# Graph network kernel: four fixed edge tiles for each of the 30 keys of the three-relation graph, counted without loops

## The reference

```python
seg = edge_type * n + dst
agg = jax.ops.segment_sum(x[src], seg, num_segments=N_REL * n)
cnt = jax.ops.segment_sum(ones, seg, num_segments=N_REL * n)
mean = agg.reshape(N_REL, n, -1) / jnp.maximum(cnt, 1.0).reshape(N_REL, n, 1)
h1 = jnp.einsum('rni,rio->no', mean, W_rel) + x @ W_root + b_rgcn
...
# three-relation layers: message of each edge, by relation
onehot = jax.nn.one_hot(edge_type, NUM_REL, dtype=h.dtype)
count = jax.ops.segment_sum(onehot, dst, num_segments=num_nodes)
inv = jnp.where(count > 0, 1.0 / jnp.maximum(count, 1.0), 0.0)
msg = xw[edge_type, src] * inv[dst, edge_type][:, None]
agg = jax.ops.segment_sum(msg, dst, num_segments=num_nodes)
```

## Time and profile before

| what | us |
|---|---|
| median of 3 runs | 1991.13 (1988.38 to 1992.34) |
| the profiled execution: its own time | 1990.38 |
| its span, first to last instruction | 1988.7 |
| 17 list units (262 to 586) | first loop of the block |
| 15 key units (588.3 to 990.6) | 402.2 |

### The profile page before, as it was taken

The page is one execution under the profiler, slowest core; times in us unless marked ns, Lnnn a source line. Parts: engine busy times, 40 slices in busy tenths (PEclk is TensorE's granted clock), DMA queues, the critical chain, the costliest instruction groups (busy, mean ns, idle before and its releaser), DMA issues. The chain is left out here.

```text
span 1988.7 us, 31024 instructions
## 1 busy us (share of the span) xinstructions
PE 1710.9 (86%) x10102; PEld 1570.3 (79%) x10103; DVE 1150.2 (58%) x1890; ACT 629.2 (32%) x839; POOL 352.4 (18%) x301
## 2 busy tenths in 40 slices
PE   2765279999989888888873998999998999899988
PEld 1643269899878777777763898899998999899988
DVE  7979777777766545555563646355343455444463
ACT  3000135565554444444443221222112222222220
POOL 5020136456452322222230000000000000000000
PEclk9876589999999989989995999899998999999999
DMA  4000249798885666666564111222012221231111
GB/s 151 24 17 0 85 156 271 209 270 261 213 260 160 157 166 183 191 174 185 162 165 120 47 49 53 81 81 72 22 55 72 72 71 32 58 84 55 50 47 47
DMA packets 84489, 230.08 MB, mean 116 GB/s; under 512 B 10350, under 2 KB 22641, under 8 KB 84434
## 3 DMA queue, kind: packets, MB, share of 16 engines
q1 hardware_dynamic: 65090, 158.14, 25.0%
q0 software_dynamic: 19344, 71.18, 15.5%
HBM read 190.01 MB, written 39.28 MB: 115 GB/s over the span
## 5 line engine op out<-in xcount | busy, mean ns | idle before, releaser
L923 PE MATMUL layers_ps_o<-layers_w_hi,layers_g_hi 128*125 128x384 f32 (+1 forms) x1040 | 362.4, 348 | 4.5 <-DVE layers_w_lo L787 3.2
L924 PE MATMUL layers_ps_o<-layers_w_lo,layers_g_hi 128*125 128x384 f32 (+1 forms) x1040 | 360.7, 347 | 0.0
L925 PE MATMUL layers_ps_o<-layers_w_hi,layers_g_lo 128*125 128x384 f32 (+1 forms) x1040 | 360.3, 346 | 0.0
L948 PE MATMUL layers_ps_g<-a,h_hi 125*128 125x316 f32 x840 | 196.7, 316 | 55.2 <-DVE h_lo L409 42.3
L1856 PE MATMUL l_means_ps<-l_means_w_hi,l_means_g_hi 128*128 128x512 f32 (+1 forms) x912 | 235.4, 339 | 0.5
L1856 PE MATMUL l_means_ps<-l_means_w_hi,l_means_g_lo 128*128 128x512 f32 (+1 forms) x912 | 235.3, 339 | 0.0
L1856 PE MATMUL l_means_ps<-l_means_w_lo,l_means_g_hi 128*128 128x512 f32 (+1 forms) x912 | 234.3, 338 | 0.0
L1567 ACT CAST l_means_w_hi<-l_means_w_raw 128x768 fp32r<-128x768 f32 x209 | 174.3, 837 | 188.9 <-PE l_means_ps L1856 182.5
L1840 PE MATMUL l_means_ps<-l_means_pick,l_means_e_hi 128*128 128x256 f32 (+1 forms) x612 | 187.5, 331 | 47.7 <-issue 30.3
L1728 DVE TENSOR_TENSOR l_means_w_lo<-l_means_w_raw,l_means_w_hi 128x768 fp32r<-128x768 f32 x209 | 190.4, 953 | 37.1 <-ACT l_means_w_hi L1567 34.3
L923 PEld LDWEIGHTS layers_ps_o<-layers_w_hi,layers_g_hi 128*125 128x125 f32 x1040 | 194.0, 187 | 14.9 <-issue 5.0
(11 more groups left out here) (318 smaller groups left out, 2481.7 us busy)
## 6 DMA issues: line engine op xcount, KB each, us to landing
l_means_w_raw<-in_L_gnn_W_rel SPq DMA_DIRECT2D x210, 384.0 KB
layers_w_raw<-in_L_gnn_w_rel SPq DMA_DIRECT2D x39, 384.0 KB, 3.5
layers_w_raw<-in_L_gnn_w_rel SPq DMA_DIRECT2D x21, 448.0 KB, 3.9
layers_a_raw<-adj SPq DMA_DIRECT2D x9, 769.0 KB
layers_w_raw<-in_L_gnn_W SPq DMA_DIRECT2D x18, 384.0 KB, 5.1
l_means_list_now<-targets SPq DMA_DIRECT2D x35, 192.0 KB
layers_w_raw<-in_L_gnn_w_root SPq DMA_DIRECT2D x13, 384.0 KB, 3.9
layers_w_raw<-in_L_gnn_w_root SPq DMA_DIRECT2D x7, 448.0 KB, 3.9
```

The costliest lines, as they stand in the source:

```text
L923: t.matmul(out, g_hi[:, f, rows], w_hi[:, f, cols], start=(f == 0), stop=False)
L924: t.matmul(out, g_hi[:, f, rows], w_lo[:, f, cols], start=False, stop=False)
L925: mm = t.matmul(out, g_lo[:, f, rows], w_hi[:, f, cols], start=False, stop=(f == fc - 1))
L948: mm = t.matmul(ps_g[:, buf, at:at + PART[p]], rows[:, k, f * 128:(f + 1) * 128], a[:, k, cols], start=(k == 0 and part == 0), stop=(k == ...
```

## The change

Every key gets four tiles of 128 slots at fixed places (`LOTS = 4`, tile number 4 x key + rank / 128), so that the list has 120 tiles instead of up to 114. One-hots and matmuls of a key are four each, written out, with no register bounds and no matmuls of zeros. One DVE instruction makes `is_src` for all four tiles; there are two buffers of four tiles. The two keys of a pair are counted ahead of `f` = 4 and of `f` = 5, and ACT copies both ahead of `take_y`. If a key has more than 512 edges, a loop over further passes makes the lists and counts again for the next 512 and adds them on DVE; the number of passes is worked out on the device. The list position is now the rank within the key, so the prefix over the keys' tiles is gone. SP stores `cnt` once 33 weight loads are issued, ahead of the later ones.

```diff
-    tiles2 = E // SLOT + keys + 1
+    tiles2 = LOTS * keys
+    room = LOTS * SLOT
+    passes_max = (E + room - 1) // room
...
-        is_src = sb("is_src", [SLOT, ONEHOTS, NP], F16)
-        is_dst = sb("is_dst", [SLOT, ONEHOTS, HALF], F16)
+        is_src = sb("is_src", [SLOT, 2, NP, LOTS], F16)
+        is_dst = sb("is_dst", [SLOT, 2, LOTS, HALF], F16)
...
+            def store_counts():
+                sp.dma_start(second.adj.rearrange("(t k) p c -> p (t k) c", t=second.kinds),
+                             cnt.rearrange("p (t a) c -> p t (a c)", a=2)).then_inc(adj_stored, 16)
+
+            def load_units(first, end):
+                with sp.Fori(first, end) as u:
+                    load(nc.s_assert_within(u, 1, units - 1, skip_runtime_bounds_check_because="as above"), False)
+
             end = count(sp)
-            with sp.Fori(1, end + 1) as u:
-                load(nc.s_assert_within(u, 1, units - 1, skip_runtime_bounds_check_because="as above"), False)
-
+            split = w_rel.shape[0]
+            load_units(1, split)
             sp.wait_ge(key_copied, keys + 1)
-            sp.dma_start(second.adj.rearrange("(t k) p c -> p (t k) c", t=second.kinds),
-                         cnt.rearrange("p (t a) c -> p t (a c)", a=2)).then_inc(adj_stored, 16)
+            store_counts()
+            load_units(split, end + 1)
+            sp.wait_ge(adj_stored, 16)
+            with sp.Fori(1, count_passes(sp)) as n:
+                p = pass_number(n)
+                sp.wait_ge(key_copied, keys * p + keys + 1)
+                store_counts()
+                sp.wait_ge(adj_stored, 16 * p + 16)
+                sp.sem_inc(waited, 1)
             sp.wait_ge(w_loaded[fc - 1], 16 * end + 16)
             sp.sem_inc(waited, 1)
-            sp.wait_ge(adj_stored, 16)
...
             def copy_key(k):
-                act.wait_ge(key_counted, k + 1)
+                act.wait_ge(key_counted, k + 3)
...
                 if key_pair is not None:
-                    copy_key(key_number(2 * key_pair))
+                    for b in range(2):
+                        copy_key(key_number(2 * key_pair + b))
...
                 if_third(act, third, take_y)
-                if key_pair is not None:
-                    copy_key(key_number(2 * key_pair + 1))
...
-                then(v.tensor_scalar(total_i[:], ps_b[0:EP, 256 + keys:256 + 2 * keys], float(SLOT - 1), None, ALU.add))
-                then(v.tensor_scalar(total_i[:], total_i[:], 7, None, ALU.logical_shift_right))
-                then(v.tensor_scalar(tiles_f[:], total_i[:], 1.0, None, ALU.max))
-                then(v.tensor_tensor_scan(tiles_end[:], tiles_f[:], zero[:].broadcast_to([EP, keys]), 0.0, ALU.add, ALU.add))
-                then(v.tensor_tensor(base[:], tiles_end[:], tiles_f[:], ALU.subtract))
-                then(v.tensor_copy(counts[0:1, 0, :], base[0:1, :]))
-                then(v.tensor_copy(counts[0:1, 1, :], tiles_f[0:1, :]))
-
-                then(v.scalar_tensor_tensor(before[:], base[:], float(SLOT), ps_b[0:EP, 256:256 + keys], ALU.mult, ALU.add))
-                then(v.tensor_scalar(before[:], before[:], 1.0, None, ALU.subtract))
...
+                then(v.tensor_reduce(most[:], ps_b[0:1, 256 + keys:256 + 2 * keys], AX_X, ALU.max))
+                then(v.tensor_scalar(passes[:], most[:], 1.0 / room, (room - 1) / (2 * room), ALU.mult, ALU.add))
+                then(v.tensor_scalar(passes[:], passes[:], 1, None, ALU.max))
+                then(v.tensor_scalar(before[:], ps_b[0:EP, 256:256 + keys], 1.0, None, ALU.subtract))
...
+                then(v.tensor_copy(rank[:], place[:, 0:EC]))
+                tiles_of_edges(then)
+                dve.wait_ge(consts_ready, 10)
+
+            def tiles_of_edges(then):
+                then(v.tensor_copy(pos_i[:], rank[:]))
                 then(v.tensor_scalar(hi_i[:], pos_i[:], 7, None, ALU.logical_shift_right))
                 then(v.tensor_scalar(lo_i[:], pos_i[:], SLOT - 1, None, ALU.bitwise_and))
                 then(v.tensor_copy(hi[:], hi_i[:]))
                 then(v.tensor_copy(slot_of[:], lo_i[:]))
-                dve.wait_ge(consts_ready, 9)
-
-            def columns(n):
-                dve.wait_ge(columns_used, n + 1)
+                then(v.tensor_scalar(over[:], hi[:], float(LOTS), float(tiles2), ALU.is_ge, ALU.mult))
+                then(v.scalar_tensor_tensor(over[:], key[:], float(LOTS), over[:], ALU.mult, ALU.add))
+                then(v.tensor_tensor(hi[:], hi[:], over[:], ALU.add))
...
-            def key_onehots(k):
-                first, end = tiles_of(dve, k)
-                with dve.Fori(first, end) as n:
-                    i = tile_number(n)
-                    dve.wait_ge(onehots_free, i + 1)
-                    at = bass.ds(i, 1)
-                    v.tensor_scalar(is_src[:, i % ONEHOTS, :], node_iota[:, 0:NP], slot_src2[:, at], None, ALU.is_equal)
-                    v.tensor_scalar(is_dst[:, i % ONEHOTS, :], node_iota[:], slot_dst2[:, at], None,
-                                    ALU.is_equal).then_inc(onehots_ready, 1)
+                dve.wait_ge(lists_taken, 2 * p + 2)
+                dve.sem_inc(waited, 1)
+
+            def key_onehots(k, b, before=0):
+                dve.wait_ge(key_counted, k + before + 1)
+                at = slot_src2[:, bass.ds(LOTS * k, LOTS)]
+                v.tensor_tensor(is_src[:, b], node_iotas[:], at.unsqueeze(1).broadcast_to([SLOT, NP, LOTS]), ALU.is_equal)
+                for j in range(LOTS):
+                    ins = v.tensor_scalar(is_dst[:, b, j, :], node_iota[:], slot_dst2[:, bass.ds(LOTS * k + j, 1)], None,
+                                          ALU.is_equal)
+                ins.then_inc(onehots_ready, 1)
...
+            dve.wait_ge(key_copied, keys + 1)
+            with dve.Fori(1, count_passes(dve)) as n:
+                p = pass_number(n)
+                dve.wait_ge(adj_stored, 16 * p)
+                done = [0]
+
+                def then_again(ins):
+                    done[0] += 1
+                    ins.then_inc(pass_step, 1)
+                    dve.wait_ge(pass_step, PASS_STEPS * p - PASS_STEPS + done[0])
+
+                then_again(v.tensor_scalar(rank[:], rank[:], float(room), None, ALU.subtract))
+                tiles_of_edges(then_again)
+                assert done[0] == PASS_STEPS
+                dve.sem_inc(waited, 1)
+                with dve.Fori(0, list_units) as n:
+                    columns(n, list_units * p)
+                take_lists(p)
+                with dve.Fori(0, key_units) as n:
+                    for b in range(2):
+                        k = key_number(2 * n + b)
+                        key_onehots(k, b, keys * p)
+                        dve.wait_ge(key_counted, keys * p + k + 3)
+                        at = cnt[:, bass.ds(k, 1), :].rearrange("p a c -> p (a c)")
+                        v.tensor_tensor(at, at, ps_b[0:NP, 0:HALF], ALU.add).then_inc(key_copied, 1)
...
-            def count_key(k):
-                pe.wait_ge(key_copied, k + 1)
-                t.matmul(ps_b[0:NP, 0:2], zeros[:, 0:NP], zeros[:, 0:2], start=True, stop=False, skip_group_check=True)
-                first, end = tiles_of(pe, k)
-                with pe.Fori(first, end) as n:
-                    i = tile_number(n)
-                    pe.wait_ge(onehots_ready, i + 1)
-                    t.matmul(ps_b[0:NP, 0:HALF], is_src[:, i % ONEHOTS, :], is_dst[:, i % ONEHOTS, :],
-                             start=False, stop=False, skip_group_check=True).then_inc(onehots_free, 1)
-                t.matmul(ps_b[0:NP, 0:2], zeros[:, 0:NP], zeros[:, 0:2], start=False, stop=True, skip_group_check=True)\
-                    .then_inc(key_counted, 1)
+            def count_key(k, b, before=0):
+                pe.wait_ge(key_copied, k + before + 1)
+                pe.wait_ge(onehots_ready, k + before + 1)
+                for j in range(LOTS):
+                    mm = t.matmul(ps_b[0:NP, 0:HALF], is_src[:, b, :, j], is_dst[:, b, j, :],
+                                  start=(j == 0), stop=(j == LOTS - 1), skip_group_check=True)
+                mm.then_inc(key_counted, 1)
...
-                        if f == fc - 1 and key_pair is not None:
-                            count_key(key_number(2 * key_pair))
+                        if f >= fc - 2 and key_pair is not None:
+                            count_key(key_number(2 * key_pair + f - (fc - 2)), f - (fc - 2))
...
             with pe.Fori(0, key_units) as n:
                 one_unit(unit(n + list_units), n)
-                count_key(key_number(2 * n + 1))```

[...]

```order
L1412 ISA
L1412 TENSOR_LOAD l_means_counts
L1412 ISA x2
L1812 UNCONDITIONAL_BRANCH
L1812 ISA
L1815 ISA [waits s0_sort_o_taken]
L1815 REGISTER_ALU
L1815 MATMUL l_means_ps<-l_means_is_dst,l_means_is_src 125x315
L1812 ISA
L1812 COMPARE_AND_BRANCH
L1817 MATMUL l_means_ps<-l_means_zeros 125x2
L1876 REGISTER_ALU
```

(52 more changed lines are left out.)

16 lines of the change are left out of this document (10 added, 6 removed).

## The result

| | median us | runs, us |
|---|---|---|
| before | 1989.76 | 4, 1987.48 to 1992.34 |
| after | 2109.1 | 4, 2108.05 to 2110.78 |

A forecast was written before the change was run, and what follows sets the result against it. PE alone was taken to bound the block. Key units -67.4, lists +0.4, positions 0 and block's end -4 gave -71 us, from 1990.38 to 1919.4, with the runs' median 0.75 higher: 1920 us; range 1906 to 1944.

The forecast's parts named there:

- rival 4: A further pass behind the last unit, from a key's 513th edge: about 150 us more, 2070 us; chance 0.03.
- The key units' sum: The 15 key units on PE take 334.8 us instead of 402.2, 67.4 us less.
- The new wait: PE waits for ACT's copy of the first key once in each key unit: 1.45 us, bounds 1.3 to 1.7.
- what hides the unit's end: At a key unit's end, 2.67 us queued on PE cover 1.78 us of branch and register work: no idle time.
- The first unit's stall: PE's 4.55 us idle in the first key unit was kept, 7.5 us more than usual; it might vanish or grow.
- the jump over the three-tile form: Jump ahead of the first key unit's matmuls, not removed by the edit, so that unit's 7.5 us extra was kept.
- Lists and positions: Longer lists in 17 units cost 0.4 us more; position work on DVE at the start was taken at 0.
- the new iota: POOL's new 500-element constant, 2.0 us, could hold DVE's compare beside it: 2 us, taken as 0.
- The block's end: Storing `cnt` a unit earlier gains 4 us at the block's end, bounds 0 to 10.
- the late loads ahead of the last `take_y`: Loads queued behind the early store, split by ACT ahead of its last `take_y`, can eat the gain: bound 0.
- Rival 1: Clock falls to half at the new wait in each key unit: 24 us more, 1944 us; chance 0.12.
- Rival 2: Key unit ends stay bare, next unit starts late and the clock falls: 49 us more, 1969 us; chance 0.08.

The follow-up runs named there:

- experiment 2: Changed kernel with the number of passes written as the constant 1, pass loops kept: 2110.09 us in one run.
- experiment 3: Changed kernel without the three pass loops, their bodies and the number of passes: 1924.45 us, ratio 0.9663 to the kernel before.
- experiment 1: Changed kernel with each of the three pass loops under a branch on `passes - 1`: 1923.68 us, ratio 0.9658 to the kernel before.
- 8: Kernel of experiment 3 with the store of the counts behind all weight loads, as before: 1920.36 us, ratio 0.9645 to the kernel before.
- experiment 6: Kernel before with its tile loops kept, keys counted ahead of product steps 4 and 5, both copies ahead of `take_y`: 2021.89 us, ratio 1.0155.
- 9: Changed kernel with guarded pass loops, first key's copy ahead of the split awaiting product step 4, store behind all loads: 1899.28 us, ratio 0.9537 to before.

## Why the prediction was wrong

**The step that failed** is rival 4's condition, "It decides from the 513th edge of one key". I worked out the number of passes, found one, and read a loop from 1 to 1 as empty. It is not: the body ran once with equal bounds (experiment 2). The lists quoted ahead of the prediction held a warning: in the order of before, whose first list is the end of a key unit in the two-tile form on PE's queue (`s0_sort_o_taken` is the semaphore `onehots_ready`), the tile loop of line 1812 and the load loop of line 1465 have their compare only behind the body. A key always has a tile and a unit a load, so before this never mattered. With that read, rival 4 was not 3 in 100 but certain.

**Its price** was set at 150 us and is 185. List groups come every 4.17 us, not 2.8, since DVE waits for the five matmuls of the last before it starts the next, 1.40 us each time (and those take 1.20 us at a clock of 0.50, 0.69 in the list unit at 306.33); 17 are 70.4 us with the gap to the first key, not 48. A key takes 3.4 us, not 2.5: 99.9 us, not 75. PE's 16.3 us of idle time ahead of them were not in the sum. The second store and what follows took 24.6 us where the block's end without a pass takes 27.1. With 0.7 us from the last key to that store, 16.3 + 70.4 + 99.9 + 0.7 + 24.6 - 27.1 = 184.8, and the next layer's first load stands 1175.56 - 990.82 = 184.7 us later than in experiment 3.

**The key units' sum** was right to 3 us (334.8 against 332.0), in the changed kernel itself. The new wait was taken at 1.45 and is 1.25 us; what hides the unit's end, 2.67 against 1.78 us, holds. The first unit's stall stayed, with 4.00 us against 4.55 before; that unit took 25.1 us, 5.6 more than the others of its form, where 7.5 was taken, and this is the largest part of the 3 us. That the stall comes from the jump over the three-tile form was my guess: no run removed that jump. What the traces show is that PE's queue has no record in it and that one packet of 0.02 MB of the DMA queue "instruction" falls in it (between 591 and 592 us before, 590 and 591 after); no run ties the two together.

**Lists and positions** were right at nothing: the first key unit starts at 587.97, 588.32 before. The compare did meet the new iota, and was not held: it took 2.82 us, as long as before, where it started behind the iotas. Before:

```profile
234.59 0.41 POOL L1519 IOTA l_means_node_iota<- 128x315 f16 x1
...
235.10 2.82 DVE L1649 TENSOR_TENSOR l_means_cnt<-l_means_key_iota,l_means_key 125x2550 f16<-125x2550 f32 x1
```

and after:

```profile
234.41 1.18 POOL L1534 IOTA l_means_node_iotas<- 128x500 f16 x1
```
```profile
234.55 2.82 DVE L1664 TENSOR_TENSOR l_means_cnt<-l_means_key_iota,l_means_key 125x2550 f16<-125x2550 f32 x1
```

**The block's end** was wrong too: 4 us gained was taken, and nothing was gained. With the early store the load comes 26.0 (experiment 1) and 27.1 us (3) after the last product, against 26.1 before and 24.0 in 8. Two steps failed. The store was read as the last thing that SP waited for; but the same view shows a wait for the other engines behind it, and POOL's last instruction of the block shows why (waits of SP before; records of line 1296):

```profile
SPq L1296 <- PEq L1296: 1.7, 1, 1.7
```
```profile
L1296 POOLq DRAIN  x1: 5907/5907/5907, 1052.3 to 1052.3; - x1
```

SP had the store behind it at 1056.5, POOL ended at 1058.2, so the store was not the last thing. And the late loads ahead of the last `take_y`, which the prediction named, were bounded at 0 instead of letting them cost. Some 4 us did come free behind the last scatter (13.0 us from the end of its issue to the load in 3, 16.8 before), but that end came 14.1 us after the last product in 3, 9.3 before.

**Rival 1** fell: the clock is 1.00 across the new wait (from 635 to 646 us). **Rival 2** fell: no key unit ends in idle time. In experiment 6 its mechanism was seen all the same, with loops kept: there PE's queue does its register work after the wait (first record at 646.5 us, wait over at 646.46). **Without the pass** the kernel takes 1924 us, 4 above the point forecast and inside the range. In the spans (1922.5 against 1988.7, 66.2 us less) the key units give 69.6 (402.2 to 920.29 - 587.66 = 332.6), the start of the block 0.7; the block's end takes 1.0 back, the two plain units 0.9 and the later layers 2.2. Of the 4 us missing, the block's end is the largest part: 4 us forecast as gained, 1.0 lost. That the rest came so near is in part luck: the key units gave 2.2 us more than forecast, and the plain units and later layers, taken at nothing, cost 3.1.

## What to carry to other kernels

Where a loop has bounds from a register, look whether a compare is executed ahead of the body. Here none was, the loop from 1 to 1 ran its body once (185 us), and the case that should do nothing needed a branch of its own. Three such branches cost nothing that shows (1923.68 against 1924.45 us). Tell an edit's form from its place: here fixed tiles without loops at the old places gave 91 us, and moving the keys cost 24 of them. A store moved up a queue can delay what stood behind it, also work whose result nobody uses: here ACT waited 13.2 us for such loads, and the next layer's load came 3.1 us later (27.1 against 24.0 us after the last product, experiments 3 and 8).

## What the runs showed of the hardware

- The pass loops with equal bounds in registers ran once, on PE, DVE and SP alike: 185 us (2109.1 against 1924.45 us; also in experiment 2, 2110.09 us).
- In the changed kernel one idle piece of 1.25 us in the 19.5 us unit left the granted clock at 1.00 (635 to 646 us). In experiment 6 pieces of 1.25, 1.80, 0.30 and 0.29 us, with single matmuls between, were followed by 0.50 (651 to 654 us).
- The same store of 2307 KB held SP for 22.8 us in the second pass, with DVE busy for 8.9 of 23 us and PE, ACT and POOL not at all (1151 to 1174 us), and for 34.5 and 34.9 us beside the scatters and the last loads (experiments 8 and 9).
- POOL's last instruction of the block, a DRAIN behind its scatters, took 5.9 us in every kernel profiled here. It ended the block before (1058.2 us), and with the early store in experiments 1 and 3 (from 984.5 and 984.0 us on).
